# Two graph layers on one core: where the list expansion, the list selection and the row store stand in the block schedule

## The reference, cut to what matters

```
h   = relu(layernorm(x))
Wh  = h @ W;   src = Wh @ a[:128];   dst = Wh @ a[128:]
att = softmax(where(adj > 0, leaky_relu(src + dst.T, 0.2), -9e15), axis=1)
hp  = att @ Wh
gi  = hp @ w_ih.T + b_ih;   gh = h @ w_hh.T + b_hh        # three parts of 128 each
r, z = sigmoid(gi_r + gh_r), sigmoid(gi_z + gh_z);   n = tanh(gi_n + r * gh_n)
x1  = x + (1 - z) * n + z * h
h2  = relu(layernorm(x1));   g = h2 @ W1.T + b1
out = x1 + adj @ g
```

## Time and profile before

| what | value |
|---|---|
| median of three runs | 1554.25 us |
| the profiled execution's own time | 1554.3 us |
| its span, first to last instruction | 1552.8 us |
| TensorE busy (matmul / weight load) | 870.6 / 601.1 us |
| VectorE busy | 1063.9 us |
| ScalarE busy | 688.0 us |
| GpSimd busy | 813.8 us |
| mean granted TensorE clock | 0.727 of full |

### The profile page before, as it was taken

How to read it: one execution, slowest core, us unless ns; L and a number is a source line. 1 busy time by engine, 2 the same in 40 slices (tenths; PEclk the granted TensorE clock), 3 DMA queues, 4 the chain that set the end, 5 groups by cost and what they waited for, 6 DMA issues and landing times.

```text
span 1552.8 us, 16240 instructions
## 1 busy us (share of the span) xinstructions
PE 870.6 (56%) x4555; PEld 601.1 (39%) x4555; DVE 1063.9 (69%) x3642; ACT 688.0 (44%) x834; POOL 813.8 (52%) x818
## 2 busy tenths in 40 slices
PE   5466566575665756657566575666624343343433
PEld 5233334343443434434344443445423333333333
DVE  7557686787867878678786787876645555555554
ACT  5735545555455554555545555452323233222221
POOL 7346534454344543445434454444167777777774
PEclk9767888888788877888778887786855555555555
DMA  9999786787866878768787687841056666666674
GB/s 368 267 389 367 275 308 241 264 317 286 318 259 259 318 290 309 269 256 315 296 311 268 251 315 288 311 172 40 20 210 225 225 224 224 228 230 234 215 246 129
DMA packets 72866, 401.19 MB, mean 258 GB/s; under 512 B 15169, under 2 KB 41026, under 8 KB 52290
## 3 DMA queue, kind: packets, MB, share of 16 engines
q1 hardware_dynamic: 51138, 357.03, 59.7%
q0 software_dynamic: 20480, 42.48, 11.8%
q10 hardware_dynamic: 1152, 0.59, 0.1%
HBM read 387.35 MB, written 12.68 MB: 258 GB/s over the span
## 4 chain that ended last, share of the span: by engine, by line
DVE 37%; PE 35%; issue 18%; POOL 4%; ACT 3%; DMA 2%; SPq 0%; DVEq 0%; ACTq 0%
PE ACC L1057 12%; DVE Y L670 11%; PE ACC L1179 10%; PE ACC L1085 5%; DVE KS L678 4%; DVE H L927 3%; DVE H L794 3%; PE GP L1121 2%; PE GP L1124 2%; POOL H L409 2%; ACT H L503 1%; POOL H L457 1%; DVE KR L683 1%; ACT hpT L560 1%; DVE WG L857 1%
## 5 line engine op out<-in xcount | busy, mean ns | idle before, releaser
L409 POOL DMA_INDIRECT H<-projected_rows,IDX x320 | 394.2, 1232 | 321.1 <-DVE IE L763 233.3
L457 POOL DMA_INDIRECT H<-layer_rows,IDX x320 | 307.0, 959 | 104.5 <-issue 104.5
L503 ACT ACTIVATE H<-X 128x4096 uint8<-128x4096 uint32 x96 | 346.4, 3609 | 11.8 <-DMA X<-in_adj_dram 9.9
L1057 PE MATMUL ACC<-Y,DW 128*128 128x512 fp8e4 x768 | 264.6, 507 | 149.7 <-DVE Y L670 110.2
L1179 PE MATMUL ACC<-H 128*128 128x128 f32 x640 | 158.2, 434 | 254.2 <-issue 196.8
L1179 PEld LDWEIGHTS ACC<-H 128*128 128x128 f32 x640 | 141.3, 329 | 271.1 <-issue 231.7
L619 ACT ACTIVATE H<-X 128x4096 uint8<-128x4096 uint32 x32 | 115.7, 3617 | 283.6 <-DMA X<-in_adj_dram 283.6
L670 DVE TENSOR_SCALAR Y<-X 128x4096 fp8e4<-128x4096 f32 x96 | 224.9, 2347 | 18.2 <-DMA X<-in_adj_dram 18.2
L1057 PEld LDWEIGHTS ACC<-Y,DW 128*128 128x128 bf16 x768 | 87.0, 122 | 277.6 <-DVE Y L670 115.4
L750 DVE TENSOR_TENSOR KK<-POSC,ACC 128x10 f32<-128x10 f32 x32 | 5.3, 166 | 211.6 <-PE ACC L1085 211.6
L935 DVE TENSOR_TENSOR H<-ACC,WG 128x128 f32<-128x128 f32 x64 | 18.7, 292 | 186.6 <-PE ACC L1179 186.6
(11 more groups left out here) (186 smaller groups left out, 1540.9 us busy)
## 6 DMA issues: line engine op xcount, KB each, us to landing
X<-in_adj_dram SPq DMA_DIRECT2D x160, 2048.0 KB, 11.0
H<-projected_rows,IDX POOLq DMA_INDIRECT x320, 7.2
H<-layer_rows,IDX POOLq DMA_INDIRECT x320, 3.2
projected_rows<-WG SPq DMA_DIRECT2D x16, 262.0 KB, 8.8
H<-in_xb_dram SPq DMA_DIRECT2D x8, 512.0 KB, 8.2
R<-in_xb_dram SPq DMA_DIRECT2D x32, 128.0 KB, 8.8
layer_rows<-GT SPq DMA_DIRECT2D x32, 128.0 KB, 1.8
out_dram<-H SPq DMA_DIRECT2D x32, 128.0 KB, 1.8
```

Of the source, the lines that this page charges most:

```text
L409: nc.gpsimd.indirect_dma_start(GB[q % 3][:, e, :], None, tab_d, bass.IndirectOffsetOnAxis(ap=IDX[:, 2 * KT5 * q + e:2 * KT5 * q + e + 1], ...
L457: nc.gpsimd.indirect_dma_start(GR[t % 6][:, e, :], None, g_d, bass.IndirectOffsetOnAxis(ap=IDX[:, KT5 * t + e:KT5 * t + e + 1], axis=0)).t ...
L503: nc.scalar.activation(J8, Xu[h % 4], ACT.Sign, accum_out=NZ[:, h:h + 1]).then_inc(a_nz, 1)
L1057: ins = nc.tensor.matmul(V[u], DW[:, 8 * side(h) + k, :], half_row[:, k * GROUPS:(k + 1) * GROUPS], start=(d == 0 and k == 0), stop=False, ...
```

## The change

The diff is the whole change. On TensorE `expand(n-1)` goes ahead of the third codes and of the gates. On VectorE `select(n-1)` goes behind the fourth map and behind the one-hots. On SyncE's queue the row store leaves its place between the loads and is the first step of the next slot; the number of slots grows by one for it, and in the added slot the other engines do nothing.

```
-        SLOTS_N = NS + 6
+        SLOTS_N = NS + 7
...
                 for n in range(SLOTS_N):            # SyncE
+                    if 0 <= n - 7 < NS:
+                        g_store(n - 7)
                     for h in (4 * n + 4, 4 * n + 5):
...
                         rows_load(n - 2)
-                    if 0 <= n - 6 < NS:
-                        g_store(n - 6)
...
                         update(n - 5)               # VectorE
-                    if 0 <= n - 1 < NS:
-                        select(n - 1)
                     if n < NS:
                         ones_of(4 * n + 3)
                     if 0 <= n - 3 < NS:
                         onehot(n - 3)
+                    if 0 <= n - 1 < NS:
+                        select(n - 1)
                     if 0 <= n - 4 < NS:
                         gate_sum(n - 4)
...
                         normed(n - 6)               # TensorE
+                    if 0 <= n - 1 < NS:
+                        expand(n - 1)
                     if n < NS:
                         codes(4 * n + 2)
                     if 0 <= n - 4 < NS:
                         gates(n - 4)
-                    if 0 <= n - 1 < NS:
-                        expand(n - 1)
                     if 0 <= n - 6 < NS:
                         projected(n - 6)
```

## The result

The changed kernel takes 1544.19 us (median of four runs, 1543.78 to 1544.95) against 1554.31 for the kernel before, timed beside it: ratio 0.9935, 95% interval 0.9917 to 0.9952. It is 10 us faster where 39 were forecast, and lies outside the range of 1494 to 1534.

The account below looks back on a forecast made before the run. The order of work was taken to bound the first part, with select waiting for expand. 14 x (4.1 - 1.5 - 0.2) = 33.6, plus 3 and 2.7, gave 39.3 off 1554.3: 1515 us, range 1494 to 1534.

Parts of the forecast that it names:

- What bounds the kernel: First part: the order of work, not an engine; VectorE's select waits 211.6 us in 32 times for TensorE's expand.
- TensorE, odd slot: Expand ahead of the third codes pushes the gates back; WE ready at 23.6, slot 29.75 against 29.54, 0.2 lost.
- TensorE, even slot: Expand and codes fit while gates wait for hpT at 22.1; WE stays at 25.0, before DX's lateness is added.
- third rival: Even slots: gates slip behind expand and codes, select's wait becomes one for WE, nothing gained, 1554; 4 in 100.
- 33.6 forecast for slots 4 to 31: Saving over 14 pairs of slots: 4.1 in even slots, less 1.5 for late DX and 0.2 in odd slots.
- VectorE: Fourth map and diagonal fill idle time at no cost; one-hots 2.55, select 2.2, gate sum and own rows 1.3 follow WE.
- GpSimd: Later select delays the gather, maps hold its issues; in even slots DX comes at 16.9, L1063 1.5 late, passed on to WE.
- The compare doesn't hold an issue: GpSimd's gather: the forecast took it that the compare holds no issue; the contrary, in a rival at 20 in 100, gave 1529.
- The row store: SyncE's queue: moving the store frees loads, but VectorE never waits for a load in these slots; worth 0.
- Slots 1 to 3 and the tail: Slots 1 to 3, with full DMA queues, save 3 (bounds 0 and 8); slot 32 onward saves 2.7 (bounds -3 and 4).

Follow-up runs that it names:

- e5: The changed kernel with three all-zero-weight matmuls of 512 columns added ahead of L1063's wait for DX in even slots; 1500.10 us, ratio 0.9647.
- e1: The changed kernel with the last four of a gather's ten issues put behind own_columns of the next slot; 1504.70 us, ratio 0.9679.
- e4: The changed kernel with the third codes ahead of expand and the gates behind both; 1503.75 us, ratio 0.9672.
- e6: The kernel before with the row store alone moved; 1553.96 us, ratio 0.9998.
- e10: The kernel before with expand alone moved, and DX of even slots held back by nine chained IOTAs on GpSimd; 1543.66 us, ratio 0.9927.

## Why the prediction was wrong

By its own steps:

- **What bounds the kernel**: right. One wait, and the order of work around it; expand's move alone brings 118 us.
- **TensorE, odd slot**: right. WE forecast for 23.6, and the slot at 29.75; measured 23.1 and 29.3.
- **TensorE, even slot**: here it failed. The step reads "expand and codes (2.2 + 1.8) from about 17.4 are done at 21.4. So the gates don't move". Both durations were taken from the kernel before, where in this slot codes and expand ran at full clock. They took 4.1 and 3.4, gates started at 26.2 of the slot (557.35) and not at 23.6 (22.1 plus the 1.5 of lateness), and WE came at 29.5 instead of 26.5. So the gates no longer wait for hpT (2.7 us in 3 times, before 42.9 in 18), which the prediction had named as the sign of its third rival. The even slot is 2.9 longer than forecast (35.6 for 32.7), times 14 that is 41 us; the odd slot is 0.45 shorter than forecast, 6 us in all. Of the 33.6 forecast for slots 4 to 31 1.5 came. e5, where in the steady slots the clock is up again behind the wait and DX just as late, is 44 faster, e1 and e4 about 40.
- **VectorE**: right but for what it rests on. Fourth map and diagonal cost nothing; one-hots, select and the rest behind WE took 6.1 (560.67 to 566.74) for 6.05 forecast. L794 waits 6.6 where about 4 was forecast, because WE is late.
- **GpSimd**: right in mechanism and nearly in size: three held issues, DX forecast at 16.9, there at 16.6 by the start of L1063; 1.2 late for 1.5. The compare doesn't hold an issue: the tenth ended at 547.15, while the compare ran from 546.25 to 547.47. But its price was put at its own length. WE comes 4.5 later than in the kernel before (29.5 for 25.0): 1.2 for the lateness, and 3.3 more through the clock.
- **The row store**: right, 0.
- **Slots 1 to 3 and the tail**: 5.6 and 3.4 for 3 and 2.7.

Of the rivals the third was nearest: "the third codes end at 21.4 against 22.1; if they ended 4 later, nothing is left". They ended at about 26.2, 4.8 later (1.2 of it by DX), and next to nothing was left. It had 4 in 100, because nothing in it said what could make them late. The rows for it were in the trace of the kernel before: codes take 3.6 just ahead, in the second codes of the same slot, and 1.97 after; the granted clock differs between two stretches 4 us apart. The sum used each duration as if it belonged to the operation, where it belonged to the place. That both of these operations would meet the half clock couldn't be read from those rows; that the clock had to be asked for could.

And the larger thing was in the prediction's own numbers as well. The forecast worked out the sum of three moves and never the worth of each. By its own numbers, expand alone gives a slot of 23.6 or 25.0 + 0.1 + 2.55 + 1.3, that is 27.5 and 29.0; 14 pairs of 56.5 instead of 64.8 are 116 us, for 118 measured. The nearness is in part luck: the pairs there take 56.0 to 58.0, 57.0 on the mean of slots 8 to 29, and slots 1 to 3 and the tail bring the rest.

## What to carry to other kernels

Work out each move of a change by itself as well as all together: a move that fills an idle stretch and one that puts the same work behind that stretch undo each other. When work is moved on TensorE, look up the granted clock of the stretch it goes to, and work the sum out at both levels where the move puts a wait just ahead of it or light matmuls first in line: both what is moved and what follows can run at half speed. A place where a step only just fits (0.7 us here) deserves more than 4 chances in 100.

## What the runs showed of the hardware that was not expected

- After a wait of 1.4 us at 1.2 GHz, with 20 light matmuls first behind it, TensorE stayed at 1.2 GHz for 8 us more though it was busy all the time (549.85 to 558.2). With eight matmuls of 512 columns first behind the same wait it rose 3.7 us after the wait (e4), and with useless matmuls in the wait it was up before expand (e5). The same light matmuls without the wait ran at full clock in e1; in six of thirteen even slots the clock fell behind them all the same (1.00 in 343.6 to 346.0, 0.50 in 346.3 to 349.7), without a wait of TensorE between.
- So useless work can pay: three matmuls of 512 columns with zero weights in 15 slots made the kernel 44 us faster than without them.
- A gather issue on GpSimd that starts within a VectorE map (128x4096 f32 to fp8, 2.3 us), or up to half a us before it, is held until the map ends: 2.4 to 3.0 us for 0.94 in the changed kernel (530.65: 2.91, map from 531.15). An issue that meets the map only at its own end isn't held (543.17: 0.97, map from 544.05). Beside the one-hots and the compare, also one f32 source, issues took 0.94 to 1.05 in these two kernels; these are short instructions (a one-hot 0.3 to 0.5 us, most compares 0.5), so a hold by one of them would be short too. A two-element power on GpSimd (L416) took 2.74 us under a map (551.41; 0.72 in the kernel before).
- Four kernels with different work in a pair of slots (the kernel before, the changed one, e6, e10) take 64.8 us for it, and two others (e4, e5) 61.4 to 61.5; why stays open.
